# A four-pass 2D GRU scan: projection split over two steps, output units on straight quadrants, border pieces, fourteen end tiles

## The reference

```
seq   = gn(x) projected from 192 channels to D = 64, for each pixel      (Wi, bi)
x_g   = seq @ W_ih.T + b_ih          h_g = h @ W_hh.T + b_hh             (three gates of 64)
r, z  = sigmoid(xr + hr), sigmoid(xz + hz)
n     = tanh(xn + r * hn)            h = (1 - z) * n + z * h             (128 steps in each direction)
out   = x + (right + down + left + up) @ Wo.T / 4 + bo                   (64 to 192 channels)
```

## Time and profile before

| what | value |
|---|---|
| median of three runs | 2590.5 us |
| the profiled execution's own time | 2584.7 us |
| its span, first to last instruction | 2582.6 us |
| PE, DVE, ACT, POOL busy | 87%, 79%, 62%, 59% |
| mean of the granted PE clock | 0.989 |
| DMA, whole span | 509 MB, mean 197 GB/s |

### The profile page before, as it was taken

The page is one execution under the profiler, slowest core; times in us unless marked ns, Lnnn a source line. Parts: engine busy times, 40 slices in busy tenths (PEclk is TensorE's granted clock), DMA queues, the critical chain, the costliest instruction groups (busy, mean ns, idle before and its releaser), DMA issues.

```text
span 2582.6 us, 79658 instructions
## 1 busy us (share of the span) xinstructions
PE 2255.1 (87%) x30544; PEld 1419.1 (55%) x30544; DVE 2053.0 (79%) x4910; ACT 1602.1 (62%) x3374; POOL 1534.0 (59%) x2108
## 2 busy tenths in 40 slices
PE   0679999999979999898979999899979999999886
PEld 0345555555546655555546665555546666555564
DVE  8239999777769999787859999788857777898854
ACT  0236666666657777666647777666657777666600
POOL 2026666667756666566656666566667766666600
PEclk9999999999989999999989999999999999999999
DMA  9973333246768786589977776589974544244299
GB/s 364 276 213 94 99 94 87 79 133 207 244 196 232 209 228 181 157 241 281 311 249 204 216 233 173 156 248 278 308 228 127 129 130 116 79 127 129 60 381 390
DMA packets 331354, 509.23 MB, mean 197 GB/s; under 512 B 36704, under 2 KB 145632, under 8 KB 330208
## 3 DMA queue, kind: packets, MB, share of 16 engines
q1 hardware_dynamic: 313248, 478.28, 63.3%
q10 hardware_dynamic: 17728, 25.85, 2.7%
HBM read 352.98 MB, written 151.01 MB: 195 GB/s over the span
## 4 chain that ended last, share of the span: by engine, by line
PE 38%; ACT 21%; DVE 20%; issue 12%; DMA 5%; SPq 4%; POOL 0%; DVEq 0%; POOLq 0%
PE bank L776 23%; ACT bank L585 8%; DVE r L896 7%; ACT z L581 6%; ACT r L577 6%; PE bank L756 5%; DVE h L910 5%; DMA work<-x 4%; PE bank L684 4%; DVE bank L901 4%; SPq L326 3%; PE bank L777 3%; DVE r L891 2%; PE bank L758 1%; DVE bn L1021 1%
## 5 line engine op out<-in xcount | busy, mean ns | idle before, releaser
L776 PE MATMUL bank<-h,wh 64*64 64x256 f32 x6144 | 1510.3, 384 | 120.1 <-DVE h L910 119.4
L756 PE MATMUL bank<-seq,wx 64*64 64x256 f32 x6144 | 1551.0, 385 | 62.6 <-DMA seq<-seq_next 23.2
L758 PE MATMUL bank<-seq,wx 64*64 64x256 f32 x6144 | 1551.8, 385 | 0.0
L777 PE MATMUL bank<-h,wh 64*64 64x256 f32 x6144 | 1518.4, 386 | 0.5 <-issue 0.5
L475 POOL TENSOR_TENSOR v<-z,h 128x256 f32<-128x256 f32 x1024 | 747.6, 730 | 782.9 <-ACT z L581 780.5
L776 PEld LDWEIGHTS bank<-h,wh 64*64 64x64 f32 x6144 | 730.4, 133 | 519.5 <-PE bank L758 301.1
L756 PEld LDWEIGHTS bank<-seq,wx 64*64 64x64 f32 x6144 | 742.1, 132 | 361.9 <-DVE r L896 210.9
L483 POOL TENSOR_TENSOR hsum<-hsum,h 128x256 f32<-128x256 f32 x1024 | 751.6, 734 | 101.1 <-DVE h L910 79.3
L758 PEld LDWEIGHTS bank<-seq,wx 64*64 64x64 f32 x6144 | 740.8, 132 | 13.9
L891 DVE SCALAR_TENSOR_TENSOR r<-bank,bhh,r 128x256 f32<-128x256 f32 x1024 | 491.4, 480 | 321.4 <-ACT r L577 268.4
L777 PEld LDWEIGHTS bank<-h,wh 64*64 64x64 f32 x6144 | 731.8, 133 | 0.1
(11 more groups left out here) (97 smaller groups left out, 2468.0 us busy)
## 6 DMA issues: line engine op xcount, KB each, us to landing
work<-x SPq DMA_DIRECT2D x832, 128.0 KB, 3.9
work<-x SPq DMA_DIRECT2D x192, 384.0 KB, 4.2
out<-work SPq DMA_DIRECT2D x576, 128.0 KB, 2.5
work<-x SPq DMA_DIRECT2D x128, 512.0 KB, 5.4
work<-x SPq DMA_DIRECT2D x32, 768.0 KB, 6.2
seq_next<-work SPq DMA_DIRECT2D x48, 512.0 KB, 5.9
work<-hsum_last SPq DMA_DIRECT2D x48, 512.0 KB, 6.0
seq<-x SPq DMA_DIRECT2D x32, 512.0 KB, 14.4
```

What stands on the lines that cost most here:

```text
L756: pe.matmul(as_pair(ps[LOW, :], c), wx[HIGH, gate, :], px[HIGH], start=start, stop=False, skip_group_check=True)
L758: return pe.matmul(as_pair(ps[HIGH, :], c), wx[LOW, gate, :], px[LOW], start=start, stop=False, skip_group_check=True)
L776: pe.matmul(ps[LOW, 0:N2], wh[LOW, gate, :], state[LOW], start=start, stop=True, skip_group_check=True)
L777: return pe.matmul(ps[HIGH, 0:N2], wh[HIGH, gate, :], state[HIGH], start=start, stop=True, skip_group_check=True)
```

## The change

1. **Projection.** `project_low` is gone. `project_straight` does the half of the low channels that goes low to low and high to high, in the straight quadrants beside `x_n` and `x_z` of the same step. `project_crossed` does the other half in the crossed quadrants beside `h_r` and `h_n` of c = 1 of step t+1, or, where step t+1 has a tile of its own (steps 71, 78, 85, 92, 99, 106, 113, 120), at the end of the same step. ACT's `project_next` and the store of the sequence follow at the new ends (`project_ends`); the last tile, begun in step 125, ends in step 126.
2. **Units.** All sums parts are straight (`unit_half`), all x parts crossed (`unit_x_half`); unit 1's two images change lanes accordingly and a bias tile per unit (`bo_unit`, four more small loads) replaces `bo_low`. 63 units are ended by ACT, one in each of steps 3 to 65; the other 33 by DVE, in steps 73 to 124, in steps without a tile and in ten steps with one (74, 79, 85, 90, 95, 100, 106, 111, 116, 121), where both halves come at the end of the step. A tile's x is loaded and its result stored by two DMAs of 384 KB in place of six of 128 KB.
3. **Border pieces.** The last ring is four pieces, `BORDER`, each with a fetch and a dump of its own. Piece 0 is fetched at step 125. The dumps stand ahead of the next scan's chunk loads. PE waits for pieces 1 and 2 ahead of the first x part and for 0 and 3 ahead of the first x part of c = 1. POOL makes v of step 0 first and clears between the first v's and the first additions.
4. **Tail.** Fourteen slots: three in the projection's x slots (loaded in steps 0 to 2 of g = 3), eight in bands of `seq` (seven of them loaded in steps 113 to 121), three in the units' x slots.

The diff, cut to its core:

```diff
-    TSLOTS = 10
+    TSLOTS = 14
+    EDGE = 32
...
     project_at = {PROJECT_FROM + 7 * m // 4: m for m in range(TILES)}
+    project_ends = {t if t + 1 in project_at else t + 1: m for t, m in project_at.items()}
...
+    ACT_UNITS_UNTIL = 66
+    unit_at = {t: t - 3 for t in range(3, ACT_UNITS_UNTIL)}
+    N_ACT = len(unit_at)
+    N_DVE = UNITS - N_ACT
+    crowded = [t for t in project_at][2::3]
+    for t in range(S_BIAS + 1, T):
+        if len(unit_at) < UNITS and (t not in project_at or t in crowded):
+            unit_at[t] = len(unit_at)
+    assert len(unit_at) == UNITS and max(project_ends) < T and max(unit_at) + 1 < T and N_ACT % 3 == 0
...
+    BORDER = [(slice(1, NB), slice(8, 16)), (slice(0, 1), slice(16, HH)), (slice(0, 1), slice(0, 16)),
+              (slice(1, NB), slice(0, 8))]
+    BORDER_STEPS = [(120, 124), (T, 120), (T, T), (T, T)]
+    FIRST_BORDER_AT = 125
...
+        xe = [xp[:, s] for s in range(XPS)]
+        xe += [seq[:, b, EDGE:HH, :].rearrange("p r w -> p (r w)").rearrange("p (k n) -> p k n", k=3)
+               for b in reversed(range(NB))]
+        xe += [xf[:, s] for s in range(XFS)]
+        last_read = [max(T - 1 - BW // 2 * b, T - 1 - EDGE // 2) for b in reversed(range(NB))]
+        xe_at = {}
+        for s in range(XPS):
+            xe_at.setdefault(s, []).append(s)
+        for s, step in enumerate(last_read):
+            if step < T - 1:
+                xe_at.setdefault(step + 2 + (s if step + 2 + s < T and s < 6 else 0), []).append(XPS + s)
...
+            def fetch_border(g, i):
+                for c in range(2):
+                    sp.wait_ge(x_z_ready[c], T * g + BORDER_STEPS[i][c])
+                stored = TILES // 2 * (g + 1) - (i == 0)
+                for a in range(2):
+                    sp.wait_ge(stage_stored[a], 16 * ((stored + 1 - a) // 2))
+                blocks, rows = BORDER[i]
+                sp.dma_start(seq[:, blocks, rows, :], seq_next[:, blocks, rows, :]).then_inc(border_fetched[i], 16)
+            def dump_border(g, i):
+                for c in range(2):
+                    sp.wait_ge(h_added[c], T * g + BORDER_STEPS[i][c])
+                blocks, rows = BORDER[i]
+                sp.dma_start(hsum_last[g % 2][:, blocks, rows, :], hsum[:, blocks, rows, :])\
+                  .then_inc(border_dumped[i], 16)
...
+                for a in range(2):
+                    src = x_px[2 * (g - 1) + a, :, px].rearrange("(k c) n -> c k n", k=3)
+                    sp.dma_start(xf[image_lanes(a, n)[1], k % XFS], src).then_inc(xf_loaded[k % XFS], 16)
...
+            def load_last(i):
+                s = i % TSLOTS
+                if i >= TSLOTS:
+                    sp.wait_ge(xe_stored[s], 48 * (i // TSLOTS))
+                elif s < XPS:
+                    sp.wait_ge(xp_used, TILES * (PAIRS - 1))
+                elif s < XPS + NB:
+                    for c in range(2):
+                        sp.wait_ge(x_z_ready[c], T * (PAIRS - 1) + last_read[s - XPS] + 1)
+                else:
+                    k = s - XPS - NB
+                    sp.wait_ge(xf_stored[k], 32 * ((TILES * (PAIRS - 1) + XFS - 1 - k) // XFS))
+                load_x(xe[s], PAIRS - 1, i, xe_loaded[s])
...
                         fetch_seq(g, fetch_at[t])
+                    if not more and t in xe_at:
+                        for i in xe_at[t]:
+                            load_last(i)
+                            issued.append(i)
+                    if more and t == FIRST_BORDER_AT:
+                        fetch_border(g, 0)
                 if more:
-                    fetch_seq(g, 3)
+                    for i in (1, 2, 3):
+                        fetch_border(g, i)
+                    for i in (1, 0, 2, 3):
+                        dump_border(g, i)
             for i in range(TILES):
...
+                if i >= TSLOTS or i not in issued:
+                    load_last(i)
...
+                make_v(g, 0, 0)
+                make_v(g, 0, 1)
                 if g > 0:
-                    pool.wait_ge(hsum_dumped[3], 16 * len(square_pieces(3)) * g)
-                    for blocks, rows in clear_after:
-                        clear(blocks, rows)
+                    clear_border(g, 1)
+                make_v(g, 1, 0)
+                if g > 0:
+                    for i in (0, 2, 3):
+                        clear_border(g, i)
                 pool.wait_ge(hsum_cleared, NB + CLEARS * g)
-                for t in range(T):
+                add_h(g, 0, 0)
+                make_v(g, 1, 1)
+                add_h(g, 0, 1)
+                add_h(g, 1, 0)
+                make_v(g, 2, 0)
+                add_h(g, 1, 1)
+                make_v(g, 2, 1)
+                add_h(g, 2, 0)
+                add_h(g, 2, 1)
+                for t in range(3, T):
...
-            def project_low(pair, m):
+            def project_straight(pair, m, side):
                 k = TILES * (pair - 1) + m
-                pe.wait_ge(high_ready, k + 1)
-                for side in range(2):
-                    pe.matmul(blocked(next_ps[HIGH], side), wa[:, :], half(xp[:, k % XPS, 0, :], side), start=False,
-                              stop=True, skip_group_check=True)
-                    last = pe.matmul(blocked(next_ps[LOW], side), wb[:, :], half(xp[:, k % XPS, 1, :], side),
-                                     start=False, stop=True, skip_group_check=True)
-                last.then_inc(xp_used, 1)
+                if side == 0:
+                    pe.wait_ge(high_ready, k + 1)
+                pe.matmul(blocked(next_ps[HIGH], side), wa[HIGH, :], half(xp[HIGH, k % XPS, 0, :], side), start=False,
+                          stop=False, skip_group_check=True)
+                last = pe.matmul(blocked(next_ps[LOW], side), wb[LOW, :], half(xp[LOW, k % XPS, 1, :], side),
+                                 start=False, stop=False, skip_group_check=True)
+                if side == 1:
+                    last.then_inc(straight_ready, 1)
+            def project_crossed(pair, m, side):
+                k = TILES * (pair - 1) + m
+                if side == 0:
+                    pe.wait_ge(straight_ready, k + 1)
+                pe.matmul(blocked(next_ps[HIGH], side), wa[LOW, :], half(xp[LOW, k % XPS, 0, :], side), start=False,
+                          stop=True, skip_group_check=True)
+                last = pe.matmul(blocked(next_ps[LOW], side), wb[HIGH, :], half(xp[HIGH, k % XPS, 1, :], side),
+                                 start=False, stop=True, skip_group_check=True)
+                if side == 1:
+                    last.then_inc(xp_used, 1)
...
                     h_r(g, t, 1)
                     if m is not None:
                         project_high(g + 1, m, 0)
...
+                    if ends is not None:
+                        project_crossed(g + 1, ends, 0)
+                    if beside_state:
+                        unit_x_half(g, u, 0)
                     h_n(g, t, 1)
...
                     if t + 1 < T:
                         x_r(g, t + 1, 0)
                     h_z(g, t, 1)
                     if t + 1 < T:
                         x_n(g, t + 1, 0)
-                    if straight:
-                        straight_half(g, u, 0)
+                    if m is not None:
+                        project_straight(g + 1, m, 0)
+                    if beside_input:
+                        unit_half(g, u, 0)
                     if t + 1 < T:
                         x_z(g, t + 1, 0)
-                    if straight:
-                        straight_half(g, u, 1)
                     if m is not None:
-                        project_low(g + 1, m)
+                        project_straight(g + 1, m, 1)
+                    if beside_input:
+                        unit_half(g, u, 1)
+                    if u is not None and not beside_input:
+                        for side in range(2):
+                            unit_half(g, u, side)
+                    if m is not None and t in project_ends:
+                        for side in range(2):
+                            project_crossed(g + 1, m, side)
```

More of the change, by code:

```diff
@@ L78, in gru_scan_2d_kernel @@
     finish_tile_of = [j if k == 0 else TILES - 1 - j for j in range(TILES // 2) for k in range(2)]
-    unit_at = {}
-    for t in range(3, T):
-        u = len(unit_at)
-        if t < SIDE_BY_SIDE:
-            free = t % 8 > 0
-        else:
-            free = t > S_BIAS and (t not in project_at or u % 3 != 1)
-        if u < UNITS and free:
-            unit_at[t] = u
-    assert len(unit_at) == UNITS and max(project_at) + 2 < T
+    ACT_UNITS_UNTIL = 66
[7 more added lines that the diff above has]
+    assert len(unit_at) == UNITS and max(project_ends) < T and max(unit_at) + 1 < T and N_ACT % 3 == 0
     unit_step = {u: t for t, u in unit_at.items()}
-    N_ACT = sum(1 for t in unit_at if t < SIDE_BY_SIDE)
-    N_DVE = UNITS - N_ACT
     x_back_at = {unit_step[3 * n] - 4: n for n in range(TILES)}
```

(40 more changed lines are left out.)

100 lines of the change are left out of this document (36 added, 64 removed).

## The result

The changed kernel takes 2525.4 us (median of 4 runs, 2524.0 to 2529.3) and the kernel before 2591.0 beside it (4 runs, 2584.6 to 2592.8): a ratio of 0.9755, 95% interval 0.9742 to 0.9768, faster by 66 us. The forecast was 2519 us. On the profiled executions it was -69 us, and measured were -60.4, from a span of 2582.6 us to one of 2522.2.

A forecast was written before the change was run, and what follows sets the result against it. The prediction took a recurrence passed between engines, 4.11 us a step, as the bound; stage, pair-change and tail terms (-12.3-10.1-9.1-1.5-17.1-19) gave -69 us, forecast 2519 us, stated range 2497 to 2545.

The forecast's parts named there:

- Free slots: Projection steps: 64x64 matmuls on free array quadrants cost nothing, so 24 of 32 steps fall from 4.67 to 4.11 us.
- the rule that the prediction cites: Different row tiles cannot access one PSUM bank simultaneously; serialised straight pairs would give 2582 us, chance 0.02.
- Doubles: Eight projection steps with the crossed half appended: PE waits for its own completion, 4.87 us each, bounds 4.45 to 5.1.
- the gate at 637.1: Estimated end of a double step: ACT waits for the last crossed record, then the gate follows; taken as 4.87 us.
- the -12.3: Steps 71 to 127 of g=0: 48 x 4.11 + 8 x 4.87 = 236.2 us against 248.5.
- x late in g=1, 2: Steps 71 to 127 there: waits for the projection's x add 7 us, range 2 to 16, giving 251.7 us twice.
- the 244.7 of regular steps: Scheduled time of steps 71 to 127 in g=1, 2, summed by step kind, before waits for x.
- rival 2: DMA takes the gain back: x 3 us later at every fourth tile of g=1, 2, about 2560 us; chance 0.11.
- Change of pair: Steps 127, 0, 1: step 127 stays at 12.7 us, bound by the store's landing; -7.1, -7.6, -2.4 us.
- POOL's block: Change of pair: clearing delayed the first v, steps 0 and 1 taking 17.2 of 29.9 us; this delay goes.
- The 1.7 us that POOL's clearing was to cost in step 1: Change of pair: clearing makes a v about 2 us late, step 1 1.7 us longer, bounds 0 and 5.
- Tail: After the last scan: ten tiles loaded ahead leave 42.5 MB at 405 GB/s; -19 us, bounds -12 and -21.

The follow-up runs named there:

- experiment 7: The changed kernel with GpSimd's clears of more than 1024 words cut in two and spread over more steps: 2521.9 us, ratio 0.9754.
- experiment 1: The changed kernel with a projection tile's low channels again as four 128-row matmuls at the end of their own step: 2546.6 us, ratio 0.9847.
- after: The changed kernel itself, with the whole change, against the kernel before: 2525.4 us, ratio 0.9755.
- experiment 3: The changed kernel with each projection's last tile ended in step 125, not 126: 2506.5 us, ratio 0.9692; repeated in another series, 2520.2 us.
- experiment 4: The changed kernel with two chunk loads of the next pair's statistics issued ahead of the border dumps: 2521.0 us, ratio 0.9747.
- experiment 5: The changed kernel with no tile loaded ahead for the tail, fourteen slots kept: 2544.1 us, ratio 0.9836.

## Why the prediction was right, and where it was not

- **Free slots.** The step that carried the argument was that 64x64 matmuls on free quadrants cost nothing and 24 of 32 steps fall to 4.11. So it is: in g=0 they take 4.11, but for those behind a double (3.91), 74 (4.20), and 118 and 125 (experiment 7), and experiment 1 shows the other side. The two halves of a straight pair into one bank start within 0.01 us of each other (481.74 and 481.75), and the steps that hold them last no longer than the others. So the rule that the prediction cites from the Trainium skill (TensorEngine Tiling, Restrictions and Gotchas) does not show here as a serialisation. The page of the Trainium skill says only that such accesses can't be simultaneous; that the passes would then run one after the other was my reading of it.
- **Doubles.** The first step was right and by the mechanism named; that it was right to 0.01 us is luck, since the gate at 637.1 that the terms led to is a step of 4.81, not 4.87. The mechanism was the wait on PE's own end, then ACT's L643, then the gate. The step after it was not thought through: it gives 0.2 back, because the h part lay beside the crossed passes. In g=0 that is 8 x 0.2 = 1.6 less than forecast, and it was made up by something that I had left out, the fills (1.0), and by step 120 (0.4). Two errors of opposite sign made 236.2 come out; the -12.3 is less good than it looks.
- **x late in g=1, 2.** Over the 244.7 of regular steps I put 7 us, and found 5.7 and 1.1 (with the fills in it). So a slot that comes free 1.9 us later did not starve the projection; rival 2 is out. Stalls remain at single steps (8.42 at step 104 of g=1, and 8.16 at step 70, just ahead of the stage). In the eleven other profiles that keep the split tiles the stage of g=1 took 246.2 to 251.1, so after's 250.4 is on the long side.
- **Change of pair.** Step 127 was forecast unchanged at 12.7 with the store's landing as the bound; it took 12.5, 14.1 and 13.4, with the fetches at +3.6 (forecast +3.9), and experiment 3 moved it by moving that store. POOL's block went as forecast. What was missed is the next in line: the chunk loads, now issued behind the dumps, make DVE's statistics wait 3.0 us in g=1, and steps 0 and 1 take 11.7, not 10.1; in g=2 they take 10.3, and what is over the forecast there is step 127. The 1.7 us that POOL's clearing was to cost in step 1 comes out in step 2, as 1.4 us (g=3 of after, g=1 and 2 of experiment 4), where the table counts it under steps 2 to 71; where DVE has waited for x before, it is hidden. I had written that the dump no longer queues behind the chunks, and did not ask what queues behind the dump.
- **Tail.** Mechanism right (experiment 5: all of it), size wrong by 6 us. The mis-sized term is the rate. I took 42.5 MB at 405 GB/s, which is 105 us, and some 8 us lost at the ends; by its window the tail moves the same bytes in 120.88 us, at a mean of 352 GB/s. The 405 was no lucky window: before, the tail held 405 to 406 from 2480 to 2560. The changed one does so in no window of 20 us. From 2500 to 2520 stores alone reach 344 GB/s, though the DMA share is 0.99. In the middle PE is busy without a gap, 92 matmuls in 20 us where the earlier trace rows had 62:

```profile
2445.00:2465.00 20.00, 20.00 (x92) 16.88 (x91) 15.26 (x23) 0.00 (x0) 0.00 (x0) 1.00 1.05 398
```

And at its start it moves 256:

```profile
2401.32:2420.00 18.68, 15.48 (x81) 12.44 (x74) 10.51 (x20) 2.70 (x6) 3.70 (x6) 0.91 0.85 256
```

Against 405 throughout, before lost some 9 us in its tail and after some 16. By windows of about 20 us, start, middle and end have each some 2 us of the difference: the start, where DVE ends the first tile only at 2411 and no store can go before; the middle, at 378 to 398; and the end, without loads. Why the middle stays under 405 is open. The measured -12.7 is at the small end of my bounds, -12 to -21.
- **Total.** -69 against -60.4 on the profiles, 8.6 short: the tail is 6.3 of it, the changes of pair 2.1, the opening and steps 2 to 71 7.0 (1.4 of it POOL's clearing), and the stages from step 71 to 127 give 6.7 back, of which 6.0 are g=2 alone. That tail and steps nearly cancel is luck.

## What to carry to other kernels

When work is fitted into free slots, follow the one item that now ends later: here the last tile's store, whose move by one step was worth 4 to 5 us at each of three changes. A late operation costs only if what follows on the other engines is late too, so add up the step and the next one. And where a kernel's opening and its transfers scatter by several us, judge an edit of a few us by its own steps in the trace and repeat the kernel in another series before believing its total.

## What the hardware showed

- Passes of 64x64 matmuls start every 0.21 to 0.22 us on all four quadrants at once, each with a record of 0.38, also when straight pairs of the projection go beside crossed ones for x (481.74 and 481.75).
- A wait of PE for its own last matmul cost 0.13 us from the end of that record to the next start (482.13 to 482.26); the two starts are 0.51 apart, where passes without the wait are 0.22 apart.
- Stores alone moved 344 GB/s at a DMA share of 0.99, loads and stores mixed 378 to 398 in the middle of after's tail and 405 before.
- A zero fill on GpSimd took 1.60 us for 1792 words a partition and 0.83 for 896; the longer is more than twice a v of 256 words (0.72), and in two pieces it no longer made a v late in step 125.
- PE's granted clock was 0.86, 0.79 and 0.84 over the three changes of pair, after PE had stood still for 7.2 us in the first of them, and 0.50, the lower of its two levels (1.2 GHz), in the last 20 us, where PE had nothing to do.
